# Reordered instructions around the last tiles of an attention and feed-forward kernel: probabilities, residual sum and low parts on VectorE and ScalarE, and the adapter weights' high part in steps 6, 24 and after the loop

## The reference

```python
h = einsum('bct,bcd->bdt', x, style_w[style])        # a 32 x 32 matrix for each sequence
q, k, v = split(clip(h @ w_qkv.T, -8, 8))
q, k = layer_norm(q) * qw + qb, layer_norm(k) * kw + kb
p = softmax(q k^T / 4 + alibi, causal)               # 32 heads of 16
x = x + (p @ v) @ w_out.T
y = einsum('bsi,boi->bso', x, adapter_w[adapter])    # a 512 x 512 matrix for each sequence
shared = relu(y @ up)**2 @ down                      # 512 -> 1024 -> 512
routed = (y @ fc1 @ expert) * sum(top2(y @ gate)) @ fc2
x = x + layer_norm(shared + routed) * gamma + beta
```

## Time and profile before

| | |
|---|---|
| median of three runs | 1090.98 us (1090.39 to 1091.02) |
| the profiled execution | 1091.25 us, of which 1089.5 us span from the first to the last instruction |
| TensorE: busy, mean granted clock | 1053.9 us (97% of the span), 0.994 |
| DVE, ACT, POOL busy | 628.2, 571.7, 568.2 us |
| DMA | 166.57 MB, mean 153 GB/s |

### The profile page before, as it was taken

One profiled execution on the slowest core, in us unless ns is written; L12 is line 12 of the kernel. 1 busy time (PEld: TensorE's weight loads), 2 busy tenths in 40 slices (PEclk: granted clock), 3 DMA queues, 4 the chain that ended last, 5 costly groups with the idle time before them and its releaser, 6 DMA issues.

```text
span 1089.5 us, 29124 instructions
## 1 busy us (share of the span) xinstructions
PE 1053.9 (97%) x12012; PEld 838.1 (77%) x12012; DVE 628.2 (58%) x1050; ACT 571.7 (52%) x955; POOL 568.2 (52%) x490
## 2 busy tenths in 40 slices
PE   5999999999999999999999999999999999999994
PEld 3778788888888888888877767786877778787883
DVE  4577767676767677777765235353444445354432
ACT  3466777777777778777775316152241615142220
POOL 5665877777777777776755224132231423233331
PEclk9999999999999999999999999999999999999997
DMA  6224555555555556555577963452716244320101
GB/s 249 75 82 150 188 186 177 185 174 185 175 183 177 187 177 208 184 171 182 160 266 259 356 161 145 120 170 68 222 31 184 86 130 151 107 59 29 49 29 39
DMA packets 99987, 166.57 MB, mean 153 GB/s; under 512 B 45648, under 2 KB 46416, under 8 KB 96016
## 3 DMA queue, kind: packets, MB, share of 16 engines
q1 hardware_dynamic: 90304, 140.97, 38.7%
q0 software_dynamic: 6064, 17.05, 5.3%
q10 hardware_dynamic: 3488, 6.70, 1.8%
HBM read 98.09 MB, written 40.89 MB: 128 GB/s over the span
## 4 chain that ended last, share of the span: by engine, by line
PE 85%; DVE 3%; DMA 3%; issue 3%; SPq 2%; POOL 2%; ACT 1%; DVEq 0%; POOLq 0%
PE banks L729 22%; PE banks L946 16%; PE pair L968 13%; PE banks L780 7%; PE banks L850 7%; PE banks L961 7%; PE pair L747 3%; PE pair L811 2%; DMA w<-in_w 2%; PE banks L713 1%; PE banks L916 1%; SPq L557 1%; PE banks L792 1%; PE banks L829 1%; PE banks L866 1%
## 5 line engine op out<-in xcount | busy, mean ns | idle before, releaser
L1805 POOL TENSOR_TENSOR w_lo<-w2t,w_hi 128x2048 fp32r<-128x2048 f32 x26 | 119.4, 4593 | 76.3 <-ACT w_hi L1131 76.3
L729 PE MATMUL banks<-wqkv_hi,h_hi 128*128 128x512 f32 x384 | 154.1, 401 | 0.6 <-DVE wqkv_lo L1602 0.4
L729 PE MATMUL banks<-wqkv_hi,h_lo 128*128 128x512 f32 x384 | 149.8, 390 | 0.0
L729 PE MATMUL banks<-wqkv_lo,h_hi 128*128 128x512 f32 x384 | 149.7, 390 | 0.0
L1894 POOL TENSOR_TENSOR frstd<-fve,cst 128x1 f32<-128x1 f32 x32 | 31.9, 997 | 202.3 <-DVE fve L1738 202.3
L1870 POOL TENSOR_TENSOR u_lo<-act,u_hi 128x512 fp32r<-128x512 f32 x64 | 82.6, 1292 | 104.7 <-ACT u_hi L1344 104.7
L1731 DVE TENSOR_TENSOR total<-total,pair 128x512 f32<-128x512 f32 x32 | 22.0, 687 | 174.9 <-PE pair L968 174.9
L1436 ACT ACTIVATE total<-banks,weight 128x512 f32<-128x512 f32 x32 | 22.0, 688 | 170.4 <-PE banks L961 170.4
L946 PE MATMUL banks<-yT_hi,up_hi 128*128 128x512 f32 x256 | 100.3, 392 | 0.0
L946 PE MATMUL banks<-yT_hi,up_lo 128*128 128x512 f32 x256 | 99.7, 390 | 0.0
L946 PE MATMUL banks<-yT_lo,up_hi 128*128 128x512 f32 x256 | 99.7, 389 | 0.0
(11 more groups left out here) (182 smaller groups left out, 2637.1 us busy)
## 6 DMA issues: line engine op xcount, KB each, us to landing
w2t<-in_w SPq DMA_DIRECT2D x26, 1024.0 KB
w<-in_w SPq DMA_DIRECT2D x24, 768.0 KB, 6.9
vx<-v_hl SPq DMA_DIRECT2D x128, 68.0 KB
x1g<-x_rows SPq DMA_DIRECT2D x32, 256.0 KB, 3.7
kx<-k_hl SPq DMA_DIRECT2D x124, 64.0 KB
x_rows<-x1t SPq DMA_DIRECT2D x31, 256.0 KB, 2.4
y_rows<-ys SPq DMA_DIRECT2D x26, 256.0 KB
w<-in_w SPq DMA_DIRECT2D x24, 256.0 KB, 3.2
```

Of the source, the lines that this page charges most:

```text
L729: m = e.matmul(into, a[:, c, :], b[:, n, c, :], start=(c == 0 and k == 0), stop=(c == KC - 1 and k == 2))
L1805: e.tensor_tensor(w2_lo[:, :, :], w2t[:, :, :], w2_hi[:, :, :].bitcast(F32), ALU.subtract).then_inc(d_wlo, 1)
```

## The change

Six places are reordered. No instruction is added or taken away, but for one wait on SP that `store_x1` makes as well.

- SP, after the loop: `load_back(0, 0, 3, 4)` ahead of `store_x1(27)`, behind the same wait for the sum of tile 27.
- ACT, step 6: `high_w2(0)` ahead of `high_probs(3)` and the chunk's split.
- ACT, step 24: `high_w2(18)` right behind `high_probs(21)`; `join_planes(0)` and `high_planes(0)` ahead of `high_chunk(19)`.
- ACT, after the loop: `high_w2(25)` ahead of `join_planes(7)` and `high_planes(7)`, but still behind `high_probs(28)`.
- ACT, after the loop: `high_probs(29)` ahead of `high_o(28)`, `scale_k(31)` and `high_k(31)`.
- DVE, after the loop: `turn_probs(29)` and `add_x(27)` ahead of `low_o(28)`, and `bias_max(30)` ahead of `low_k(31)`.

```diff
             load_back(0, 1, 3, 4)
             spread_v(T - 3)
+            upto(e, "x1", T - 5)
+            load_back(0, 0, 3, 4)
             store_x1(T - 5)
-            load_back(0, 0, 3, 4)
             spread_k(T - 1)
...
+                if i == LAG:
+                    high_w2(0)
                 if i >= 3:
                     high_probs(i - 3)
+                if i == T - 8:
+                    high_w2(i - LAG)
...
-                if 0 <= i - 5 < CHUNKS:
-                    high_chunk(i - 5)
                 if i >= T - 8:
                     join_planes(i - T + 8)
                     high_planes(i - T + 8)
-                if i >= LAG:
+                if 0 <= i - 5 < CHUNKS:
+                    high_chunk(i - 5)
+                if i > LAG and i != T - 8:
                     high_w2(i - LAG)
...
             high_probs(T - 4)
+            high_w2(LAST)
             join_planes(EARLY_GROUPS * KC - 1)
             high_planes(EARLY_GROUPS * KC - 1)
-            high_w2(LAST)
...
             soft_exp(T - 3)
+            high_probs(T - 3)
             high_o(T - 4)
             scale_k(T - 1)
             high_k(T - 1, k_last)
-            high_probs(T - 3)
             slot_out(LAST, B2)
...
             divide(T - 4)
+            turn_probs(T - 3)
+            add_x(T - 5)
             low_o(T - 4)
-            add_x(T - 5)
-            turn_probs(T - 3)
+            bias_max(T - 2)
             low_k(T - 1, k_last)
-            bias_max(T - 2)
             add_x(T - 4)
```

## The result

| | median, us | range, runs |
|---|---|---|
| before | 1090.59 | 1089.65 to 1091.02, 6 |
| changed | 1094.95 | 1093.85 to 1095.20, 6 |

The ratio is 1.0037, interval 1.0027 to 1.0047. The change costs 4.4 us; I had forecast a gain of 3. The profiled execution took 1094.96 us, its span is 1093.1.

What follows compares the result with a forecast made beforehand. PE bounds the kernel with 85% of the chain, so only its idle places can give time; 0.72 + 0.50 + 0.35 + 1.42 = 2.99 us, to 1088.0 from a median of 1090.98; 80% range 1087.2 to 1089.5.

Steps and rivals of the forecast that it cites:

- the term of +0.50: Step 24: POOL done 2.78 us sooner, so PE's 0.50 us wait before the adapter product goes; bounds 0 and 0.50.
- The fetch behind the planes: After the loop: first fetch of up weights 1.8 us later, perhaps delaying kx of tile 30; term taken as 0.35, worst -1.1.
- Step 6: Weights' high part first on ACT, matrix landed by about 105.15; PE's 0.72 us wait before the adapter product goes.
- The matrix has long landed here: Step 24: the weights' matrix is already there, so ACT's high part starts at 424.75 and not at 427.53.
- This gives 0.54 of the 0.66: After the loop: of PE's 0.66 us wait before the out projection of tile 28, 0.54 goes.
- The whole 1.42 goes: After the loop: PE's 1.42 us wait before the values of tile 29, for POOL's low probabilities, goes entirely.
- 1.77: Summed gain after the loop: 0.35 at the projection of tile 28 and 1.42 at the values of tile 29.
- The transfers push back: Rival, 15%: kx of tile 30 lands late or the unexplained gap in those scores grows; gain 1.5 (1089.5), half way 2.2.
- Slower: Rival, 5%: kx of tile 31 lands late by DVE's new order, PE waits 4.7 us; 1.7 us slower, 1092.7.
- The gate product: Rival, 10%: group 1's gate product waits for low y behind the fetch stream; PE keeps 0.7 of 1.77, gain 1.9, 1089.1.
- A step does not pay: Rival, 8%: low chunk in step 24 or normalization in step 6 late; 0.5 or 0.7 us go, 1088.6.

Runs made afterwards that it cites:

- the run where POOL only writes: Changed kernel with POOL's low part of the weights of slots 18 and 25 replaced by fills of zeros of about the same length; 1090.00 us.
- step 24 alone: Kernel before with only the change of step 24: weights' high part right behind the probabilities, planes ahead of the chunk; 1093.52 us, ratio 1.0021.
- steps alone: Kernel before with step 6 as changed and step 24 in the order planes, weights, chunk, last tiles as before; 1089.68 us, ratio 0.9984.
- the tail alone: Kernel before with only the last tiles reordered on DVE, ACT and SP as in the change; 1091.33 us, ratio 1.0003.
- the mended ones: Changed kernel with ACT's old order after the loop, and in step 24 the old order (1089.63 us) or planes, weights, chunk (1089.29 us).
- low k first: Changed kernel with planes, weights, chunk in step 24, old ACT order after the loop, and DVE's low_k(31) ahead of bias_max(30); 1089.26 us.

## Why the prediction was wrong

- **The step that failed** is in step 24: "DVE takes its low part ahead of q and of the low chunk, so the low chunk moves from 429.59 to about 430.4 and ends at 431.1", which left PE 0.3 us of room. I let the low part keep its length of before. In before, POOL's low part of the weights began at about 429.5, behind it; the change starts POOL's at 426.14, ahead of it. DVE's 0.69 became 3.48, and the term of +0.50, whose lower bound I had put at 0, became a loss: 2.87 of wait and 1.2 at half clock against the 0.50. Shown by the run where POOL only writes, and by step 24 alone, 2.5 us slower.
- **The same miss after the loop.** "The fetch behind the planes" looked at what stands behind the rounding on ACT and not at what the rounding lets POOL do. The planes' low part fell under POOL's for slot 25 (3.54 us, wait 2.34). The late fetch of the up weights did come, at 555.94 in place of 551.28, of which 2.9 us are PE's own lateness and the rest the 1.8 that I had named. No wait there ended on it: kx of tile 30 was on time, with PE late as well. So what the late fetch would have cost PE on time is not shown.
- **Step 6 was right:** the matrix landed by 104.26, sooner than my 105.15; the 0.72 is gone, and 0.89 came out at slot 0 (0.14 of it stood already at 84 us, ahead of step 6). No DVE instruction with two SBUF inputs was held there. **The 0.50 of step 24 was real** as well, with the planes ahead: steps alone -1.5 us. But "The matrix has long landed here" was not so: in the changed kernel ACT waits 0.25 us for it, until 424.14.
- **The tail was mis-sized.** Of "This gives 0.54 of the 0.66" nothing came in the changed kernel (0.64 is left), and 0.47 with the tail alone. "The whole 1.42 goes" was right for the wait and wrong for the time: 1.77 summed, 0.1 slower by the medians with the tail alone. The 1.42 had hidden the wait for the next piece of program, which now shows in the values of tile 29 as 0.88; what took the rest of the 1.77 is not shown by any run. Where a shift took the gap out of the values of tile 28, kx of tile 30 waited instead. In the changed kernel, where PE comes 5.3 us late to the tail, 1.65 do come out from slot 25 to PE's end; that this is so because data and program had by then arrived is argued, not shown.
- **The rivals.** "The transfers push back" came nearest for the tail, but neither of its two events came with the tail alone: kx of tile 30 is not late, and the gap in those scores did not grow. The gap in the values of tile 28 stays, at 0.7 us in the changed kernel and 1.3 and 1.6 us in two of the mended ones. "Slower" by kx of tile 31 is there as a wait of 1.0 us (I had 0.4 of room), and is gone with low k first, without any change of the time. The gate product was no limit. "A step does not pay" names the instruction that came late, the low chunk in step 24, but prices it at the 0.5 that would not come; it cost 2.87 of wait. That an instruction on DVE grows longer by the weights' move stood in no rival.

## What to carry to other kernels

When an operation is moved on one engine, follow what it releases: the long POOL instruction that starts sooner must be laid over DVE's row, and every DVE instruction with both inputs in SBUF that comes under it must be costed up to POOL's end. Then let such DVE instructions go first and release POOL behind them: planes, weights, chunk gave what weights, planes, chunk lost. And before a wait of the matrix engine is counted as a gain, ask what it hides; here pieces of program and a transfer were due in the same 10 us.

## What the runs showed that I had not expected

- A DVE subtraction of 128x512 with both inputs in SBUF took 3.48 and 3.54 us under a POOL subtraction that reads SBUF, and 0.69 under POOL's fills. It ended about 0.55 us after POOL's subtraction in all five cases. With one input in PSUM (the low chunk) it took 0.69 under the same POOL instruction.
- Behind waits of 2.3 to 3.2 us TensorE's granted clock was 0.50 for about 3 us or 7 us, or (once, at 2.34) did not fall. The fall made a 2.82 us product 3.91.
- Inside matmuls with no wait PE stood still for 1.01 and 1.69 us at the edge of a 16 KB piece of its program, the first in a stretch where the DMA engines moved 373 GB/s; 64 matmuls more at the start moved the place by 64 matmuls, 128 put it back. With the tail alone it stood still 0.88 us at such an edge, with 18 GB/s around its packet. It went on 1.3 to 1.5 us after the packet's end.
